# Copying the sums of an attention half out of PSUM with ACT, and normalising them from SBUF one period later

## The reference, cut to what matters

```
x = x + xattn(ctx_1024, layernorm(x))         # 1024 queries, 6404 + 1024 keys, 16 heads of 64
  q = lat @ Wq;  k, v = split(concat(norm(ctx), lat) @ Wkv)
  attn = softmax(q @ k.T * 64 ** -0.5)
  return (attn @ v) @ Wout
```

## Time and profile before

| | |
|---|---|
| time, three runs | 2425.65, 2420.95, 2423.75 us, median 2423.75 us |
| profiled execution | span 2422.2 us from the first to the last instruction; a time of its own beside the span is not recorded |
| attention stage | about 115 to 2072 us of the span |
| PE busy | 2278.6 us, 94% of the span; nine tenths or more of each slice in the attention stage |
| DVE busy | 1851.0 us, 76% |
| ACT busy | 1674.6 us, 69% |
| POOL busy | 1860.4 us, 77% |
| mean granted clock of PE | 0.978 |

### The profile page before, as it was taken

The page is one execution under the profiler, slowest core; times in us unless marked ns, Lnnn a source line. Parts: engine busy times, 40 slices in busy tenths (PEclk is TensorE's granted clock), DMA queues, the critical chain, the costliest instruction groups (busy, mean ns, idle before and its releaser), DMA issues. The chain is left out here.

```text
span 2422.2 us, 68504 instructions
## 1 busy us (share of the span) xinstructions
PE 2278.6 (94%) x27967; PEld 1476.3 (61%) x27967; DVE 1851.0 (76%) x2815; ACT 1674.6 (69%) x3028; POOL 1860.4 (77%) x1124
## 2 busy tenths in 40 slices
PE   2899999999999999999999999999999999779996
PEld 1356665566556655666566656665666665557885
DVE  8878888888788878888888788878888772348775
ACT  4677777777777777777777777777777777246663
POOL 1788899889988898889888988898889999340001
PEclk8899999999999999999999999999999999789998
DMA  2431314132413141314131413142313000240000
GB/s 89 120 81 42 95 62 121 41 92 66 117 43 95 59 119 44 93 51 122 51 92 44 124 61 92 41 115 67 92 42 106 25 2 2 87 125 1 2 2 12
DMA packets 124634, 165.68 MB, mean 68 GB/s; under 512 B 26392, under 2 KB 100192, under 8 KB 123872
## 3 DMA queue, kind: packets, MB, share of 16 engines
q1 hardware_dynamic: 122176, 157.53, 23.2%
q10 hardware_dynamic: 2144, 3.77, 0.5%
HBM read 99.28 MB, written 61.97 MB: 67 GB/s over the span
## 5 line engine op out<-in xcount | busy, mean ns | idle before, releaser
L631 POOL TENSOR_TENSOR att_prob_low<-att_prob 128x1024 f16<-128x1024 f32 x960 | 1767.0, 1867 | 191.3 <-PE all_banks L751 151.6
L908 ACT ACTIVATE att_prob<-all_banks 128x512 f32<-128x512 f32 x1888 | 1070.7, 591 | 386.2 <-PE all_banks L716 263.1
L1002 DVE TENSOR_REDUCE att_part<-all_banks 128x2 f32<-128x1024 f32 x800 | 946.7, 1218 | 195.3 <-PE all_banks L676 195.3
L737 PE MATMUL all_banks<-att_v,att_prob 128*128 128x129 f16 x5664 | 583.6, 220 | 2.9 <-DVE shared_att L1026 0.6
L737 PEld LDWEIGHTS all_banks<-att_v,att_prob 128*128 128x128 bf16 x5664 | 414.2, 98 | 237.9 <-issue 10.3
L751 PEld LDWEIGHTS all_banks<-att_v,att_prob_low 128*128 128x128 f16 x7552 | 328.6, 98 | 135.4 <-POOL att_prob_low L631 15.9
L697 PE MATMUL all_banks<-att_qc,att_kc 128*128 128x512 f16 x1056 | 401.2, 380 | 0.0
L698 PE MATMUL all_banks<-att_qd,att_kd 128*128 128x512 f16 x1056 | 401.0, 380 | 0.0
L751 PE MATMUL all_banks<-att_v,att_prob_low 128*128 128x65 f16 x7552 | 385.1, 194 | 11.4 <-POOL att_prob_low L631 11.3
L741 PE MATMUL all_banks<-att_v,att_prob 128*128 128x64 f16 x1888 | 371.1, 197 | 0.0
L739 PE MATMUL all_banks<-att_v,att_prob 128*128 128x65 f16 x1888 | 365.7, 194 | 0.0
(11 more groups left out here) (313 smaller groups left out, 3042.1 us busy)
## 6 DMA issues: line engine op xcount, KB each, us to landing
v_all<-att_stage_v SPq DMA_DIRECT2D x98, 258.0 KB, 2.7
att_kc<-k_high SPq DMA_DIRECT2D x90, 232.0 KB, 3.9
att_v<-v_all SPq DMA_DIRECT2D x28, 483.8 KB
att_v<-v_all SPq DMA_DIRECT2D x28, 451.5 KB
k_high<-att_stage_h SPq DMA_DIRECT2D x98, 128.0 KB, 1.7
k_low<-att_stage_l SPq DMA_DIRECT2D x98, 128.0 KB, 1.9
att_kd<-k_low SPq DMA_DIRECT2D x45, 232.0 KB, 4.3
att_kc<-k_high SPq DMA_DIRECT2D x30, 232.5 KB, 4.4
```

The source lines that it names most:

```text
L631: pool.tensor_tensor(prob_low[g % NL][:, 0:w], p[:, 0:w], p.bitcast(BF16)[:, 1:2 * w:2], op=ALU.subtract).then_inc(low_split, 1)
L737: pe.matmul(O[:, q, :], w, v[:, e, t, :], start=first, stop=False, skip_group_check=True)
L908: act.activation(prob[g % NP][:, i * BANK:(i + 1) * BANK], S[n % 3], ACT.Exp, scale=SCALE)\
L1002: dve.tensor_reduce(parts[:, n:n + 2], pers.banks[:, 4 + 2 * pair:6 + 2 * pair, :], axis=AX.X, op=ALU.max)\
```

## The change

`O` is no longer read by DVE. At the end of a half ACT copies the whole region, 452 columns, to a new SBUF tile `raw` (`copy_sums`). The copy stands between the first and the second exponential of the next half's first period. PE's `sums_free` waits for the copy alone. DVE's `normalize_half` moves behind the takes and the seed of that first period; it forms the reciprocals from `raw`, adds the second set of sums to the first inside `raw`, and multiplies once, from SBUF to SBUF. One multiplication, the tile `rest` and two semaphores go, a copy and two semaphores come. The copy and the normalisation of the very last half stand after the loops.

```
@@ -341,7 +341,9 @@
         nm = sc.sb("nm", [P, 2, HALF], F16)
         rden = sc.sb("rden", [P, 4])
         zeros = sc.sb("zeros", [P, P], F16)
-        rest = sc.sb("rest", [P, WIDE, DH])
+        SUM_COLS = WIDE * VCOLS + DH + 1
+        raw = sc.sb("raw", [P, 4 * VCOLS])
+        raw_o = raw[:, :].rearrange("p (j c) -> p j c", c=VCOLS)
         warm = sc.sb("warm", [1, 1])
         spare = sc.sb("spare", [P, 10])
         k_high = nc.dram_tensor("k_high", (INNER, KEYS), F16, kind="Internal").ap()
@@ -353,13 +355,14 @@
         X = [pers.banks[:, 4 + n, :] for n in range(4)]
         Y = X[0]
         O = pers.banks[:, :, :].rearrange("p b q -> p (b q)")[:, 0:4 * VCOLS].rearrange("p (j c) -> p j c", c=VCOLS)
+        sums = pers.banks[:, :, :].rearrange("p b q -> p (b q)")[:, 0:SUM_COLS]
         names = ("y_ready y_copied y_split constants filled scored exp_done low_split high_done low_done "
-                 "max_scored max_taken top_ready top_spread top_placed inverted normalized tail_ready v_ready kd_ready ident_ready rest_taken rest_added "
+                 "max_scored max_taken top_ready top_spread top_placed inverted joined normalized tail_ready v_ready kd_ready ident_ready sums_copied "
                  "nm_placed even_seeded odd_seeded").split()
         s = {n: sc.sem(n) for n in names}
         (y_ready, y_copied, y_split, constants, filled, scored, exp_done, low_split, high_done, low_done,
-         max_scored, max_taken, top_ready, top_spread, top_placed, inverted, normalized, tail_ready,
-         v_ready, kd_ready, ident_ready, rest_taken, rest_added, nm_placed, even_seeded, odd_seeded) = (s[n] for n in names)
+         max_scored, max_taken, top_ready, top_spread, top_placed, inverted, joined, normalized, tail_ready,
+         v_ready, kd_ready, ident_ready, sums_copied, nm_placed, even_seeded, odd_seeded) = (s[n] for n in names)
         kq_out = [sc.sem(f"kq_out{n}") for n in range(NR)]
         v_out = [sc.sem(f"v_out{n}") for n in range(NR)]
         NF = 8
@@ -372,7 +375,7 @@
         parts = part[:, :, :].rearrange("p j c -> p (j c)")
         FIRST_LOW = [att[:, n, BANK:BANK + BANK // 2].bitcast(F16) for n in range(NF)]
 
-        EXP0, HIGH0, LOW0, SPLIT0, NORM0, OUT0 = 2, 3, 3, 3, 1, 32
+        EXP0, HIGH0, LOW0, SPLIT0, OUT0 = 2, 3, 3, 3, 32
         MEAN_PAIR = struct.unpack('f', struct.pack('2e', 1.0 / DH, 1.0 / DH))[0]
         SIDE = PAIRS + 1
         LAST = UNITS - 1
@@ -722,9 +725,8 @@
                     pe.wait_ge(v_in[e], 16 * V_PIECES * turn)
                 elif g == 0:
                     pe.wait_ge(y_split, TASKS)
-                pe.wait_ge(normalized, NORM0 + 2 * b + g // SIDE)
                 if b or g:
-                    pe.wait_ge(rest_taken, 2 * b + g // SIDE)
+                    pe.wait_ge(sums_copied, 2 * b + g // SIDE)
 
             def apply_high(b, e, g, i):
                 pe.wait_ge(exp_done, EXP0 + place(b, g, i) + 1)
@@ -915,11 +917,22 @@
                 act.wait_ge(exp_done, EXP0 + n - 2)
                 act.activation(S[n % 3], nm[:, g // SIDE, :], ACT.Copy).then_inc(odd_seeded, 1)
 
+            def copy_sums(b, h):
+
+                act.wait_ge(low_done, LOW0 + b * UNITS + (h + 1) * SIDE)
+                if b or h:
+                    act.wait_ge(normalized, 2 * b + h)
+                act.activation(raw[:, 0:SUM_COLS], sums, ACT.Copy).then_inc(sums_copied, 1)
+
             def head(b, e, with_max, projecting, i):
                 for w in range(PERIODS):
                     last = 2 * w % SIDE == PAIRS - 1
                     n, after = place(b, 2 * w), place(b, 2 * w + 1) + len(tiles(2 * w + 1))
                     exp(n + 2)
+                    if w == 0 and b:
+                        copy_sums(b - 1, 1)
+                    elif 2 * w == SIDE:
+                        copy_sums(b, 0)
                     if not last:
                         exp(n + 3)
                     t = task_at(e, w) if projecting else None
@@ -968,6 +981,7 @@
                 exp(n)
             for b in range(HEADS):
                 head(b, b % 2, b + 1 < HEADS, b // 2 + 1 < HEADS // 2, b // 2)
+            copy_sums(HEADS - 1, 1)
 
         @block.vector
         def _(dve):
@@ -1019,17 +1033,16 @@
                    .then_inc(top_ready, 1)
 
             def normalize_half(b, h):
-                dve.wait_ge(low_done, LOW0 + b * UNITS + (h + 1) * SIDE)
-                dve.reciprocal(rden[:, :], O[:, :, DH]).then_inc(inverted, 1)
-                dve.wait_ge(inverted, 2 * b + h + 1)
+
+                n = 2 * b + h + 1
+                dve.wait_ge(sums_copied, n)
+                o = raw_o[:, 0:WIDE, 0:DH]
+                dve.reciprocal(rden[:, :], raw_o[:, :, DH]).then_inc(inverted, 1)
+                dve.tensor_tensor(o, o, raw_o[:, 0:WIDE, DH + 1:VCOLS], op=ALU.add).then_inc(joined, 1)
+                dve.wait_ge(inverted, n)
+                dve.wait_ge(joined, n)
                 o = att[:, 4 * h:4 * h + 4, dyn(b * DH, DH)]
-                dve.tensor_tensor(o, O[:, :, 0:DH], spread_columns(rden[:, :], DH), op=ALU.mult).then_inc(normalized, 1)
-                dve.tensor_tensor(rest[:, :, :], O[:, 0:WIDE, DH + 1:VCOLS], spread_columns(rden[:, 0:WIDE], DH),
-                                  op=ALU.mult).then_inc(rest_taken, 1)
-                dve.wait_ge(normalized, NORM0 + 2 * b + h + 1)
-                dve.wait_ge(rest_taken, 2 * b + h + 1)
-                o = att[:, 4 * h:4 * h + WIDE, dyn(b * DH, DH)]
-                dve.tensor_tensor(o, o, rest[:, :, :], op=ALU.add).then_inc(rest_added, 1)
+                dve.tensor_tensor(o, raw_o[:, :, 0:DH], spread_columns(rden[:, :], DH), op=ALU.mult).then_inc(normalized, 1)
 
             def head(b, e, with_max, projecting, i):
                 for w in range(PERIODS):
@@ -1045,11 +1058,12 @@
                     u = seeds_before(*next_period(b, w))
                     if u is not None and (w + 1 < PERIODS or with_max):
                         seed(place(b, 2 * w + 1) + len(tiles(2 * w + 1)) + 2, u)
-                    if 2 * w + 2 in (SIDE, UNITS):
-                        normalize_half(b, 2 * w // SIDE)
+                    if w == 0 and b:
+                        normalize_half(b - 1, 1)
+                    elif 2 * w == SIDE:
+                        normalize_half(b, 0)
 
             dve.memset(zeros[:, :], 0.0).then_inc(constants, 1)
-            dve.memset(spare[:, 1:2], 0.0).then_inc(normalized, NORM0)
             dve.memset(spare[:, 2:3], 0.0).then_inc(max_taken, 2)
             for r in range(NR):
                 dve.memset(spare[:, 4 + r:5 + r], 0.0).then_inc(kq_out[r], OUT0)
@@ -1067,6 +1081,7 @@
                     finish_max(0, 0)
             for b in range(HEADS):
                 head(b, b % 2, b + 1 < HEADS, b // 2 + 1 < HEADS // 2, b // 2)
+            normalize_half(HEADS - 1, 1)
 
 
 def stage_attention_out(nc, pers, A):
```

## The result

The changed kernel takes 2497.68 us (median of 4 runs, 2494.03 to 2501.45) against 2422.35 us for the kernel before in the same comparison (4 runs, 2418.67 to 2425.65): a ratio of 1.031, interval 1.0292 to 1.0328. The profiled execution has a span of 2499.3 us at a mean granted clock of 0.970.

The account below looks back on a forecast made before the run. PE was taken to bound the attention stage, its pauses deciding. 41 us (hold) + 27 (clock) + 2 (small terms) = 70 us, added to the median of 2423.75 us, gave 2494 us; range 2430 to 2512 us.

Parts of the forecast that it names:

- 1: `apply_high`: Start of a half: with ACT's copy, PE's `apply_high` starts 0.12 us sooner, 0.28 us at the other kind of end.
- 2: first take: Half start: normalisation no longer precedes DVE's maxima, so first take 1.28 us earlier, seed at 678.91, PE freed about 1.1 us sooner.
- Step 3: New normalisation: POOL holds DVE's SBUF multiplication, so 27 projections start 1.59 or 1.44 us late; 41 us lost.
- Step 4: PE pauses 2.5 us before 27 projections; 18 pauses bring 3.4 us at half clock, costing 1.5 us each: 27 us.
- Rival (a): Multiplication is held, but the clock stays up in almost all pauses: 41 + 2 us, 2467 us; chance 0.19.
- The order: In the normalisation, POOL's third operation of a half starts 0.11 us before DVE's multiplication, at both kinds of half end.
- rival (c): DVE's multiplication comes before POOL's third operation, POOL waits; projection 0.03 and 0.18 us earlier, 3 us, 2418 us; chance 0.19.
- Rival (b): Multiplication only slowed by POOL, projection 0.48 and 0.33 us late: 11 us, 2435 us; chance 0.14, including held at one kind only.
- Small terms: Last four halves, without projection: 1.5 us lost (-2 to +2); very last normalisation about +0.3 us; 2 us in the sum.

Follow-up runs that it names:

- pauses filled: Changed kernel, plus 36 PE matmuls of zeros before the projection's wait in the 27 places where PE pauses; 2470.15 us, ratio 1.0144 to the kernel before.
- two ways above: The changed kernel with ACT padded (2422.20 us) or with the order by semaphore (2417.22 us).
- order by semaphore: Changed kernel, but POOL waits for DVE's multiplication before its third operation of each half; 2417.22 us, ratio 0.9975 to the kernel before.
- ACT padded: Changed kernel, plus a useless 128-column ACT copy before the last exponential of each half's first period; 2422.20 us, ratio 0.9965 to the kernel before.

## Why the prediction was right

Its form and all its steps held; the count of stretches at half clock and the small terms were sized low, the hold a little high. Times for head 4's first half, with 20.59 us taken off those of after:

| step | before | predicted | measured |
|---|---|---|---|
| 1: `apply_high` | 677.46 | 677.34 | 677.33 |
| 2: first take | 678.12 | 676.84 | 676.88 |
| 2: seed | 680.19 | 678.91 | 678.95 |
| 2: PE's low pair | 680.92 | 1.1 sooner | 1.23 sooner |
| 3: addition ends | | 680.32 | 680.31 |
| 3: POOL's third operation starts | 680.44 | 680.32 | 680.31 |
| 3: multiplication starts | | 680.43 | 680.41 |
| 3: multiplication ends | | 682.51 | 682.48 |
| 3: projection starts | 682.15 | 683.74 | 683.68 |

At the other kind, the end of head 4's second half, the timeline has this row for the projection:

```profile
768.98 0.23 PE L657 MATMUL all_banks<-shared_wv_h,shared_kvh 128*128 128x128 f16 x1 [2.51 <-DVE att_part L1016]
```

- **Step 3, 41 us predicted.** At the first kind the projection is 1.53 us late (1.59 predicted). At the other, the half's window begins at 761.66 here and at 738.14 before; with 23.52 us taken off, the row above is at 745.46, 1.38 us behind 744.08 (1.44 predicted). 14 x 1.53 + 13 x 1.38 = 39.4 us, and the run with the pauses filled has 39.6.
- **Step 4, 27 us predicted.** 2.51 us for each pause against 2.5; 1.52 us for each stretch against 1.5. Mis-sized was the count: 21 stretches, where two in three, 18, had been taken. 32.0 us measured. The count rested on two pauses, one that brought the half clock and one that did not, so that it came near is in part luck. Rival (a), the clock that stays up, is refuted by the windows and by the filled pauses.
- **The order.** The margin was 0.10 to 0.11 us in 29 of the 31 inner halves, against 0.11 predicted. It decided the sign, as rival (c) said: with DVE ahead, by either of the two ways above, halves 2 to 28 are 1.3 and 4.3 us shorter than before, and (c) had 3. Rival (b), a mere slowing, is refuted: the multiplication takes 0.42 us or about 2.07, and where POOL was further ahead it took as long as POOL had left and 0.28 us more: 1.70 us in the one inner half where it started 0.48 us after POOL. In the other exception, the last inner half, it was first by 0.72 us and took 0.42.
- **Small terms, 2 us predicted.** The last four halves lost 3.9 us. Two stretches at half clock lie in them, from 1982.0 and 2087.8 us, where there had been none, and the term had no clock in it; but the run with the order by semaphore has two there as well and takes 222.8 us for these halves, as before. How much of the 3.9 us is clock stays open. (The 1.3 us in the first row of the table by stage lie ahead of the first exponential, which stands between 114.4 and 116.3 us in these runs, whatever the kernel.)

The sum: 41 + 27 + 2 = 70 us were predicted, 39.6 + 32.0 + 3.9 = 75.5 measured in these stretches of the profiles, 75.3 between the medians. The 41 was 1.4 us high and the 27 was 5 us low, so the errors cancelled in small part.

## What to carry to other kernels

A DVE operation that takes both inputs from SBUF can cost all that is left of the POOL operation beside it, so count a whole POOL operation for it unless a semaphore, and not a margin of 0.1 us, puts it first; moving data out of PSUM to free a bank can turn a cheap instruction into such a one. What POOL does itself, or ACT does, is out of the conflict. And count a stop of PE like those of 2.3 to 2.7 us here twice, once for itself and once for the clock behind it; stops of 0.50 us, and of 0.86 to 1.22 us where DVE was first, brought no half clock in halves 2 to 28.

## What the runs showed of the hardware that was not expected

A held DVE operation may wait for more than one POOL operation. In the experts stage DVE works on `hidden` (32 x 1024, one input, SBUF to SBUF) while POOL converts the next stage's context in an unbroken series. The profiled run with the order by semaphore:

```profile
2123.30 1.15 POOL L1263 TENSOR_TENSOR later_ctx_l<-later_ctx,later_ctx_h 128x512 f16<-128x512 f32 x1
...
2124.40 0.60 POOL L1249 CAST later_ctx_h<-later_ctx 128x512 f16<-128x512 f32 x1
...
2124.53 2.12 ACT L1306 ACTIVATE experts_hidden<-experts_biased 32x1024 f32<-32x1024 f32 x2 [12.12 <-DVE experts_biased L1357]
2124.53 19.45 DVE L1363 TENSOR_SCALAR experts_hidden<-experts_biased 32x1024 f32<-32x1024 f32 x1
2124.97 1.15 POOL L1263 TENSOR_TENSOR later_ctx_l<-later_ctx,later_ctx_h 128x512 f16<-128x512 f32 x1
```

One operation took 19.45 us, to 2143.98, until POOL's series, which ends at 2144.25, was all but over. The same operation took 0.98 us in the profile before, and 0.68 us in the second experts stage, with no such series beside it. A long hold is not the rule: in seven other profiles POOL's series was under way first as well, and there the operation took 0.72 to 1.07 us six times and 5.75 us once, in the changed kernel. What decides is not shown. With one input from SBUF an operation is not free of POOL, it seems. ACT did its half of the same work, two operations, in 2.12 us beside the same series. The Trainium skill, page SBUF — State Buffer, section "Who interferes with whom", says that ACT never waits for another engine, which these rows bear out, and that the first to issue keeps the other out for its whole instruction; here the other was kept out over some 25 of them.

In the two profiled runs with the largest such loss (18.5 and 20.3 us for both operations, in the run with ACT padded and in this one) the rest of the program behind the attention stage took 373.8 and 371.0 us; in the other eight it took 355.7 to 359.7. Six of these ten kernels, the one before too (7 of the 13 runs of one comparison), have runs some 15 us above their others. In the last run POOL holds its series back until DVE is done:

```
+ pool.wait_ge(s["hidden_back"], 1)
  context_high(0)
```

> The run in which POOL does the addition and the multiplication, and besides: in the experts stage POOL waits with its unbroken series of conversions and subtractions on the context until DVE's two operations on hidden are over (they were 0.98 and 1.55 us in the profile before, but 15.7 and 2.8 us, and 19.4 us for one, in the two profiled runs with the upper of the two times). If that series, once it is first, keeps DVE out until it ends, and if this is where the upper of the two times comes from: both operations take about 1 us each, no run lies some 15 us above the others, and the median is 2385 to 2398 us. If the upper level comes from elsewhere, runs at 2405 to 2412 us are still seen. If the next stage waits for the series, which now starts up to 6 us later: 2394 to 2400 us throughout.

```profile
2100.08 1.39 DVE L1378 TENSOR_SCALAR experts_hidden<-experts_biased 32x1024 f32<-32x1024 f32 x2
...
2101.60 1.17 POOL L1263 CAST later_ctx_h<-later_ctx 128x512 f16<-128x512 f32 x2 [17.66 <-DVE experts_hidden L1378]
```

Both operations together took 1.39 us, the rest of the program 355.8 us, and the four runs lie between 2390.77 and 2392.60 us; the same kernel without the wait had three between 2388.51 and 2392.84 and one at 2411.14. That this series is the cause of the upper times fits, but four runs are too few to show it, and only one execution of each kernel has a trace.
